# Eight bytes: where the moving operands of a feed-forward's matrix products begin in SBUF

## The reference, cut to what matters

```
x = layernorm(x + attention(x))        # 16 query heads, 4 key heads, pooled remote keys
t = fwht(x * SU_ug) / 64               # Hadamard transform over the 512 columns
u = t @ W_up.T * (scale_u * 64);  g = t @ W_gate.T * (scale_g * 64)      # to 2048 columns
h = fwht(silu(g) * u * SU_dp) / 64
y = h @ W_down.T * (scale_d * 64)      # back to 512 columns
x = layernorm(x + y)
```

## Time and profile before

| | |
|---|---|
| median of 3 runs | 1551.35 us (1547.98 to 1556.89) |
| profiled execution, its own time | 1548.87 us |
| its span, first to last instruction | 1547.1 us |
| TensorE matmuls, busy | 1513.5 us, 98% of the span, 11744 instructions |
| VectorE, ScalarE, GpSimd busy | 67%, 40%, 30% |
| granted TensorE clock, mean | 0.998 |
| DMA, mean | 199 GB/s |

### The profile page before, as it was taken

The page is one execution under the profiler, slowest core; times in us unless marked ns, Lnnn a source line. Parts: engine busy times, 40 slices in busy tenths (PEclk is TensorE's granted clock), DMA queues, the critical chain, the costliest instruction groups (busy, mean ns, idle before and its releaser), DMA issues.

```text
span 1547.1 us, 29636 instructions
## 1 busy us (share of the span) xinstructions
PE 1513.5 (98%) x11744; PEld 1422.1 (92%) x11744; DVE 1034.0 (67%) x1790; ACT 625.8 (40%) x1289; POOL 465.0 (30%) x580
## 2 busy tenths in 40 slices
PE   6999999999999999999999999999999999999998
PEld 5977978888887899899999999999999999999998
DVE  6876787677687886865575576566467547557645
ACT  4263245236227755533333343343343333334332
POOL 5465457438338533500220030030040022003001
PEclk9999999999999999999999999999999999999999
DMA  7031122122112796678578667767776857866862
GB/s 284 1 116 69 35 83 102 35 82 103 64 64 101 275 378 246 236 273 307 205 242 295 231 241 263 268 216 264 272 238 226 322 195 257 288 231 231 283 234 97
DMA packets 92072, 307.63 MB, mean 199 GB/s; under 512 B 9888, under 2 KB 10272, under 8 KB 90144
## 3 DMA queue, kind: packets, MB, share of 16 engines
q1 hardware_dynamic: 90928, 301.54, 54.8%
q10 hardware_dynamic: 1008, 4.20, 0.7%
HBM read 255.37 MB, written 50.33 MB: 198 GB/s over the span
## 4 chain that ended last, share of the span: by engine, by line
PE 64%; DVE 4%; ACT 1%; issue 1%; POOL 1%; POOLq 0%; DVEq 0%; ACTq 0%
PE ff_bank_b L2061 16%; PE ff_bank_a L2061 11%; PE ff_bank_c L2061 11%; PE ff_acc L2095 8%; PE ff_acc L2098 7%; PE ff_acc L2086 7%; DVE ff_d_lo L1775 2%; PE ff_x_ps L2020 1%; PE ff_x_ps L2009 1%; PE ff_x_ps L2032 1%; ACT at_union L601 1%; DVE ff_c L1826 0%; DVE ff_h_lo L1794 0%; DVE ff_c L1822 0%; DVE ff_ring L1770 0%
## 5 line engine op out<-in xcount | busy, mean ns | idle before, releaser
L2061 PE MATMUL ff_bank_b<-ff_x_hi,ff_ring 128*128 128x256 f32 x1536 | 296.8, 278 | 4.1 <-DVE ff_c L1826 3.5
L2061 PEld LDWEIGHTS ff_bank_b<-ff_x_hi,ff_ring 128*128 128x128 f32 x1536 | 246.3, 188 | 5.6 <-issue 5.4
L2061 PE MATMUL ff_bank_b<-ff_x_lo,ff_ring 128*128 128x256 f32 x768 | 212.8, 277 | 0.0
L2095 PE MATMUL ff_acc<-ff_d_lo,ff_h_hi 128*128 128x256 f32 x1008 | 199.8, 279 | 2.4 <-DVE ff_d_lo L1775 2.4
L2061 PE MATMUL ff_bank_c<-ff_x_hi,ff_ring 128*128 128x256 f32 x1024 | 200.3, 280 | 0.0
L2061 PE MATMUL ff_bank_a<-ff_x_hi,ff_ring 128*128 128x256 f32 x1024 | 199.6, 279 | 0.0
L2098 PE MATMUL ff_acc<-ff_d_hi,ff_h_lo 128*128 128x256 f32 x1008 | 197.7, 277 | 0.0
L2061 PEld LDWEIGHTS ff_bank_c<-ff_x_hi,ff_ring 128*128 128x128 f32 x1024 | 164.2, 188 | 2.2 <-issue 2.2
L2061 PEld LDWEIGHTS ff_bank_a<-ff_x_hi,ff_ring 128*128 128x128 f32 x1024 | 164.3, 188 | 0.3 <-issue 0.2
L1822 DVE TENSOR_TENSOR ff_c<-ff_bank_b,ff_c 128x512 f32<-128x512 f32 x64 | 44.3, 692 | 172.0 <-PE ff_bank_b L2061 171.1
L2095 PEld LDWEIGHTS ff_acc<-ff_d_lo,ff_h_hi 128*128 128x128 f32 x1008 | 152.9, 188 | 6.4 <-issue 6.4
(11 more groups left out here) (321 smaller groups left out, 3482.3 us busy)
## 6 DMA issues: line engine op xcount, KB each, us to landing
ff_ring<-gu_scratch SPq DMA_DIRECT2D x392, 512.0 KB, 5.1
gu_scratch<-ff_ring SPq DMA_DIRECT2D x56, 512.0 KB, 4.3
at_xt<-in_xt SPq DMA_DIRECT2D x4, 2048.0 KB, 8.0
at_xn<-in_x SPq DMA_DIRECT2D x32, 256.0 KB, 2.9
x_scratch<-at_x SPq DMA_DIRECT2D x32, 256.0 KB, 2.0
ff_raw<-in_wgu SPq DMA_DIRECT2D x8, 1024.0 KB, 7.1
at_wd_a<-in_wd SPq DMA_DIRECT2D x8, 512.0 KB, 4.0
mixed_scratch<-at_wd_a SPq DMA_DIRECT2D x8, 512.0 KB, 3.3
```

Of the source, the lines that this page charges most:

```text
L2061: i = pe.matmul(bank[:, m, :], r[:, a, m, c, :], b[:, k, c, :], start=(k < 3 and m == 0 and c == 0 and b is x_hi and a == 0), stop=(m == 1 ...
L2095: pe.matmul(acc[:, t, half], h_hi[q][:, j, k], d_lo[:, j, half], start=False, stop=False, skip_group_check=True)
```

## The change

One tile, `streamed`, takes the place of the four. It holds their 4 x 512 + 4 x 7 x 256 values and 8 more, and the four are views into it that begin after its first 2 values. So each of the four begins 8 bytes later, 72 bytes modulo 512 from the weights. `gap_behind` is 8 values shorter, so every tile behind it stays where it was. Nothing else differs: no instruction is added, removed or moved.

```diff
         sb("gap_in_front", [P, 16])
-        d_hi, d_lo = sb("d_hi", [P, 2, D], F32R), sb("d_lo", [P, 2, D], F32R)
-        x_hi, x_lo = sb("x_hi", [P, MULS, 2, HB2], F32R), sb("x_lo", [P, MULS, 2, HB2], F32R)
-        sb("gap_behind", [P, 1008])
+        streamed = sb("streamed", [P, 4 * D + 4 * MULS * HB2 + 8], F32R)[:, 2:2 + 4 * D + 4 * MULS * HB2]
+        d_hi, d_lo = (streamed[:, 2 * D * i:2 * D * i + 2 * D].rearrange("p (j n) -> p j n", j=2) for i in range(2))
+        x_hi, x_lo = (streamed[:, 4 * D + 2 * MULS * HB2 * i:4 * D + 2 * MULS * HB2 * (i + 1)].rearrange("p (k c n) -> p k c n", k=MULS, c=2) for i in range(2))
+        sb("gap_behind", [P, 1000])
         xs_hi, xs_lo = sb("xs_hi", [P, FB], F32R), sb("xs_lo", [P, FB], F32R)
```

## The result

The changed kernel takes 1595.07 us (1591.83 to 1595.08) against 1551.35 before, ratio 1.027 with a 95% interval of 1.022 to 1.032. The profiled execution went from 1548.87 to 1591.83 us, its span from 1547.1 to 1590.0: 42.9 us more. The forecast was 1539.

A forecast was written before the change was run, and what follows sets the result against it. TensorE's own pace was taken to bound the feed-forward. Putting 2,877 slow matmuls at the fast pace gave -12.8 us, other terms nothing: 1551.35 - 12.8 = 1538.6, written as 1539, with 1530 to 1577 for 8 in 10.

The forecast's parts named there:

- The bound: Feed-forward: nothing but TensorE's own pace sets the end; it is busy for 98% of the span.
- The two paces: Feed-forward matmuls: one form runs at 113.3 or 117.8 ns, 5,400 fast and 2,877 slow, each pace lasting, turning at fixed places.
- (a): Pace of the 8,277 matmuls: all go at the fast pace, a gain of 12.8 us.
- 96 bytes between the two streams: Slow-phase matmuls: the 8-byte shift raises the moving stream's lead over the weights from 88 to 96 bytes, the fast phase's.
- The bound from above: Feed-forward matmuls: all at the last down projection's pace, 120.0 ns, would cost +42.4 us.
- the tail: Slow case beyond 117.8 ns, chance 0.07, left out of the 8 in 10 range.
- the good phase is lost: Rival, long quiet stretches: fast matmuls turn slow, 1562.6 us if paces swap, 1575 if both slow; chance 0.30.
- Its condition: That rival's ground: fast phases are the exception, and a finer shift may lose the only one.
- (b): Moving rows starting off a 16-byte boundary: one more 64-byte block entered, +3.4 us at most, taken as nothing.
- (c): ScalarE and VectorE writing the four tiles at the new offset: no added time taken.
- nothing happens: Rival, matmul paces: the address has no effect and paces turn as now, 1551 us or 1555 with (b); chance 0.20.
- The attention shows no fast record: Argument for the lost-phase rival: the attention's 256-column matmuls take 279 to 280 ns, so fast phases are the exception.

The follow-up runs named there:

- c64: The changed kernel with the one tile's views begun at its first value, 64 bytes modulo 512 from the weights; ratio 1.002 to the kernel before.
- d320: One tile as in the changed kernel, moving tiles 320 bytes modulo 512 from their weights; ratio 1.0005 to the kernel before.
- d576: One tile as in the changed kernel, moving tiles 576 bytes behind the ring, 64 modulo 512; ratio 1.000 to the kernel before.
- d192: One tile as in the changed kernel, moving tiles 192 bytes modulo 512 from their weights; ratio 1.002 to the kernel before.
- (5): Three kernels, one tile as in the changed kernel, moving tiles at 80, 96 or 128 bytes from their weights; ratios 1.017, 1.018, 1.016 to the kernel before.
- (2): Weights and moving tiles all begin 8 bytes later than in the kernel before, distance 64 kept; ratio 1.021.
- d80: One tile as in the changed kernel, moving tiles 80 bytes modulo 512 from their weights; 1576.93 us, ratio 1.017 to the kernel before.
- d96: One tile as in the changed kernel, moving tiles 96 bytes modulo 512 from their weights; ratio 1.018 to the kernel before.
- shift16: Weights and moving tiles all begin 16 bytes later than in the kernel before, distance 64 kept; median 1550.57 us, ratio 1.000.
- y64: The kernel before with the transposes' operand at 64 modulo 512 from its weights, all behind it moved 352 bytes; ratio 1.005.

## Why the prediction was wrong

**The bound was right.** TensorE's pace set the end of the feed-forward, and the change could act only there: its matmuls take 47.0 us more, of which the earlier start (2.8) and the folding (1.3) give some back.

**The two paces were right, the count of them too**: 2,877 matmuls at 117.8 ns. That they last and turn at fixed places holds: c64, d320 and d576 have them at the same places, and as many within 2%. One of the readings behind it was not as stated: the DMA is a little busier in the slow stretch shown, 0.80 against 0.76. Another slow stretch, 853.0 to 891.8 us, has 0.68, so traffic still isn't the cause.

**The step that failed is (a), "I take the fast pace for all".** It rested on start times averaged to 3.3 and 2.5 ns in records of 1 ns, turned into 96 bytes between the two streams. At 72 there is no 113.3 ns pace, nor a steady 117.8; the matmuls take 117 to 124 ns. Taken in the same way, the next weight load begins 2.8 ns after its matmul in the changed kernel. That is 27 bytes, so the streams stand 99 apart, next to the 96 wanted, and the pace is 121.2. And in d192 the lead is 3.3 ns at 113.3 and at 117.8 ns alike, so this lead doesn't tell the pace. Both reasons are outside that argument: the moving row starts inside a 16-byte line, and it leaves the distance of 64 modulo 256. How the 6.2 ns divide can't be given as a sum. By the distance alone 80 and 128 cost 4.0 ns and 96 costs 5.0 (5); by the start in the line at distance 64, of weights and moving rows together, it is 5.0 (2). The two would add up to more than 6.2, so they overlap: each takes away the 113.3 ns pace, worth 2.8 ns on average (117.8 less 115.0), and adds 1.2 to 2.3 of its own. What in TensorE or SBUF makes either cost time, no run shows.

**The bound from above was nearly the answer.** All at the pace of the last down projection, 120.0 ns, was +42.4 us; measured were 43.0. That the two agree so well is partly chance. At 121.2 ns the pace alone is 8,400 x 6.2 = 52 us; some 5 of it vanish in waits, mostly the six at pair 1, and 4.1 more in the earlier start and the folding. I had a term of about the right size, from a row, and gave it to the tail. The rival "the good phase is lost" named the right side and place but stopped at 117.8 ns: 1575, 20 us short. Its condition was right, since an operand pair at another distance or start does lose the exceptional pace.

**(b) was wrong in size.** +3.4 us for one more 64-byte block was worked out on the wrong unit. The Trainium skill, "SBUF — State Buffer", section "Door 1: The DMA port swizzle", has SBUF lines of 16 bytes and a price for crossing into a new one. The runs agree with such a unit at the distance 64 (8 bytes off 120.05 ns, 16 bytes off a pace of 113.3 again). The price is far above the 0.42 ns a matmul of (b): 5 ns, with the weights off the boundary too. One line more in 64 would be 1.8 ns of 115, an estimate with that page's line of 16 bytes; no run shows that crossing into a line is what costs the time.

**(c) was right**: the writers take the same time, 783 and 624 ns against 812 and 622.

**The rival "nothing happens"** had the rule of independent ports (the Trainium skill, "SBUF — State Buffer", section "Who interferes with whom") behind it. By that rule the place of one operand relative to the other should not matter. The runs do not agree: with the same matmuls at the same clock, and all starts on 16-byte boundaries, the mean pace goes from 115.0 (c64) to 119.0 and 120.0 ns (d80, d96). That the two reads meet at a port isn't shown by this.

**One argument of the rival was weak.** "The attention shows no fast record" was true of that execution. In the changed kernel the same attention line, with nothing of it moved, goes at 113.3 ns in part: its records begin at 275 ns, against 278 before.

```profile
L108 PE MATMUL at_big<-at_xs_lo,at_wq_hi x192: 275/279/282, 30.7 to 430.8; 128*128 128x256 f32 x192
```

So in the attention the pace isn't fixed by the distances alone, and something else decides which one is entered. c64, d320 and d576 differ there too (92, 46 and 46 starts 113 or 114 ns apart, none before), while their feed-forward is like that of before. What decides stays open, and so does why only every second Hadamard product at 0 restores the pace.

## What to carry to other kernels

When TensorE is the bound, measure its pace from start to start, stretch by stretch, before and after any change of layout: a start or a distance shifted by 4 to 64 bytes cost 1 to 3% here with no instruction changed. Start moving rows and weights at multiples of 16 bytes, try a few distances on the chip, and re-time after every shift. When a pace exists in a good and a bad form, the default for an untried placement is the worst row seen, not the best: the good one is the exception that needs keeping.

## What the runs showed of the hardware that I had not expected

- A 128x128 by 128x256 fp32r matmul at the full clock has no single price: mean 115.0 ns at operand distances 64, 320 and 576, 116.9 at 192, 119.0 at 80 and 128, 120.0 at 96, 118.7 at 68, 121.2 at 72, 120.05 at 64 with both operands 8 bytes off a 16-byte boundary.
- At good distances it has two lasting paces, 113.3 and 117.8 ns (118.4 in shift16). The place of the operands of 112 matmuls, beside the 8,400, decided which (1551 against 1567 to 1570 us), and matmuls with a worse distance, 0, were the ones that restored the better one. They aren't enough for it: in y64 they stand at 0 too, and the pace is 117.8.
- Runs of the kernel before spread from 1546.8 to 1568.2 us over the experiments. The upper end is the time of a kernel wholly at 117.8 ns; that these executions were such is a guess, since none of them was profiled.
